# Second and third attention: value products in two column halves over two steps, maxima ahead of scores, outputs turned in the banks of the maxima

## The reference, cut to what matters

```python
# L1: EMBED 512, H = 32 heads, D = 16, 8 key/value heads, rope;  L2: 32 heads, D_K = 16, no rope, then a product with w_o
k = jnp.repeat(k, REP, axis=2)                                    # L1 only
scores = jnp.einsum('bqhd,bkhd->bhqk', q, k) / jnp.sqrt(jnp.float32(D))
probs = jax.nn.softmax(scores.astype(jnp.float32), axis=-1)
out = jnp.einsum('bhqk,bkhd->bqhd', probs, v).reshape(B, S, E)
```

## Time and profile before

| what | value |
|---|---|
| median of three executions | 2761.74 us |
| the profiled execution, its own time | 2762.35 us |
| its span, first to last instruction | 2760.6 us |
| TensorE busy / VectorE busy / ScalarE busy | 2230.8 / 1399.9 / 1264.6 us |
| mean granted clock of TensorE | 0.903 of full speed |
| L1 attention, its 256 steps | from 1194.87 us to 1593.45 us (last copy of O) |
| L2 attention, its 256 steps | from 1852.66 us to 2245.43 us |
| L2 attention, first and 13th copy of O | 1885.97 us, 2176.24 us |

### The profile page before, as it was taken

The page is one execution under the profiler, slowest core; times in us unless marked ns, Lnnn a source line. Parts: engine busy times, 40 slices in busy tenths (PEclk is TensorE's granted clock), DMA queues, the critical chain, the costliest instruction groups (busy, mean ns, idle before and its releaser), DMA issues. The chain is left out here.

```text
span 2760.6 us, 29801 instructions
## 1 busy us (share of the span) xinstructions
PE 2230.8 (81%) x10640; PEld 1250.1 (45%) x10640; DVE 1399.9 (51%) x1933; ACT 1264.6 (46%) x2097; POOL 630.0 (23%) x460
## 2 busy tenths in 40 slices
PE   4989999999997977478888757478888786998757
PEld 3657777777776733232222223222222233443434
DVE  3564545555552445577888163177888513103153
ACT  3545556556563222046777732017777742001321
POOL 1645655656552023200000022100000001001021
PEclk8989999999998988568999878789999988999878
DMA  4861111111112102302110002511121003000001
GB/s 106 245 206 39 46 57 54 42 57 54 43 42 89 61 22 90 77 1 36 18 26 10 1 16 91 129 17 24 30 41 24 1 16 123 0 0 0 18 12 47
DMA packets 78930, 138.70 MB, mean 50 GB/s; under 512 B 30808, under 2 KB 40792, under 8 KB 78832
## 3 DMA queue, kind: packets, MB, share of 16 engines
q1 hardware_dynamic: 78832, 137.40, 18.2%
HBM read 95.95 MB, written 41.03 MB: 50 GB/s over the span
## 5 line engine op out<-in xcount | busy, mean ns | idle before, releaser
L2139 POOL TENSOR_TENSOR l0a_p_low<-yT,l0a_p_high 128x1024 fp32r<-128x1024 f32 (+7 forms) x256 | 386.0, 1536 | 282.3 <-ACT l0a_p_high L2167 282.3
L173 POOL TENSOR_TENSOR applied<-prepared,neghalf 128x2 f32<-128x2 f32 x64 | 58.4, 913 | 1546.0 <-DVE prepared L154 1546.0
L1421 DVE TENSOR_REDUCE l2a_mx<-ps 128x2 f32<-128x1024 f32 x256 | 307.8, 1224 | 114.3 <-PE ps L1305 113.4
L1421 DVE TENSOR_REDUCE l1a_mx<-ps 128x2 f32<-128x1024 f32 x256 | 308.5, 1224 | 98.2 <-PE ps L1305 97.3
L1402 ACT ACTIVATE l1a_prob<-ps 128x512 f32<-128x512 f32 x512 | 278.0, 595 | 112.9 <-PE ps L1332 74.2
L1402 ACT ACTIVATE l2a_prob<-ps 128x512 f32<-128x512 f32 x512 | 278.0, 595 | 106.6 <-PE ps L1332 69.5
L2200 DVE TENSOR_REDUCE l0a_mx<-ps 128x1 f32<-128x512 f32 (+3 forms) x384 | 203.6, 553 | 236.2 <-PE ps L2046 145.3
L2156 ACT ACTIVATE yT<-ps 128x1024 f32<-128x1024 f32 (+7 forms) x256 | 166.3, 650 | 187.2 <-PE ps L2068 123.5
L1332 PE MATMUL ps<-l1a_q,l1a_k 49*128 49x512 f32 x512 | 135.0, 524 | 68.5 <-ACT l1a_prob L1402 64.4
L1332 PE MATMUL ps<-l2a_q,l2a_k 49*128 49x512 f32 x512 | 133.3, 518 | 69.1 <-ACT l2a_prob L1402 64.3
L2167 ACT CAST l0a_p_high<-yT 128x1024 fp32r<-128x1024 f32 (+7 forms) x256 | 172.6, 674 | 7.1
(11 more groups left out here) (297 smaller groups left out, 4233.4 us busy)
## 6 DMA issues: line engine op xcount, KB each, us to landing
l0a_q<-l0a_q SPq DMA_DIRECT2D x32, 512.0 KB, 3.3
l0q_woh<-in_l0a_wo SPq DMA_DIRECT2D x16, 512.0 KB, 5.2
l0a_q<-f SPq DMA_DIRECT2D x32, 256.0 KB, 4.6
l0a_q<-l0q_q_pe SPq DMA_DIRECT2D x32, 256.0 KB, 3.6
l0a_recip_rows<-l0a_recip_row SPq DMA_DIRECT2D x32, 256.0 KB, 3.4
l0a_o<-l0a_o_pair SPq DMA_DIRECT2D x16, 512.0 KB, 2.8
yT<-l0a_o SPq DMA_DIRECT2D x16, 512.0 KB, 3.3
l1a_q<-l1a_q_parts SPq DMA_DIRECT2D x16, 256.0 KB, 5.5
```

What stands on the lines that cost most here:

```text
L1421: nc.vector.tensor_reduce(mx[:, g % 2, :, p, qt, c], banks(("pair", m)), AX.X, ALU.max).then_inc(s_red, 1)
L2139: nc.gpsimd.tensor_tensor(p_low[:, j % 4, P * j:T], prob[:, j % 4, P * j:T], p_high[:, j % 4, P * j:T], ALU.subtract).then_inc(s_pl, 1)
```

## The change

Four things change in `attend`, for both attentions.

1. The four value products of a key tile are each cut into two of 256 columns. The first half stands in step 2j + 4 and the second in step 2j + 5, for j = 0 to 5; tile 6 has steps 16 and 17 and tile 7 has 17 and 18. So nearly each step has one half of a tile, where some had a whole one and others none.
2. In a step TensorE does the maxima first, then the turned maxima and the turned outputs where they are due, then it waits for the exponential and does the scores, then the value products.
3. The turned output goes into a pair of banks of the ring, and no more into `O`; it is a job of the ring, with its wait. It moves from step 20 to 21, and `finish` stays at 21. The next value products wait for the copy `osb` alone, no more for `finish`. The reciprocals get two buffers.
4. ScalarE copies `O` between the two exponentials of step 19, where it did so behind both.

```diff
--- before.py
+++ after.py
@@ -912,8 +912,8 @@
 EXT = MAX_ROW + 1
 AHEAD = 8
 TURN_STEP = STEPS - AHEAD + 2
-PV_STEP = (7, 8, 9, 10, 12, 14, 16, 18)
-OUT_STEP, TURN_OUT_STEP, FINISH_STEP = 19, 20, 21
+PV_STEP = [(2 * j + 4, 2 * j + 5) for j in range(6)] + [(16, 17), (17, 18)]
+OUT_STEP, TURN_OUT_STEP = 19, 21
 
 
 def rows_out(chip, name, W):
@@ -1164,7 +1164,7 @@
     mx = sb("mx", [P, 2, 2, 2, NT, 2])
     mcol = sb("mcol", [P, 4 * NT])
     mrow = sb("mrow", [4 * NT, P], F32R)
-    rden = sb("rden", [P, NT // 2, GROUP])
+    rden = sb("rden", [P, 2, NT // 2, GROUP])
     LOADS = 16 * 8
     loaded = [chip.shared(f"sa_heads_loaded{i}", LOADS * len(range(i, GROUPS, SLOTS))) for i in range(SLOTS)]
     placed = [chip.shared(f"sa_max_placed{i}", 32 * (GROUPS // 2)) for i in range(2)]
@@ -1206,6 +1206,9 @@
         if at >= 0 and at % STEPS == TURN_STEP and at // STEPS + 1 < GROUPS:
             turn_at[at // STEPS + 1] = at
             ring.append(("turn", at // STEPS + 1))
+        if at >= TURN_OUT_STEP and (at - TURN_OUT_STEP) % (2 * NT) == 0:
+            ring.append(("out", (at - TURN_OUT_STEP) // (2 * NT)))
+    ring.append(("out", GROUPS * HALVES - 1))
     ring_of = {job: r for r, job in enumerate(ring)}
 
     def banks(job):
@@ -1223,6 +1226,8 @@
         kind, n = ring[r]
         if kind == "pair":
             engine.wait_ge(s_red, b_red + n + 1)
+        elif kind == "out":
+            engine.wait_ge(s_out, b_out + n + 1)
         else:
             engine.wait_ge(s_mrow, b_mrow + n + 1)
 
@@ -1244,7 +1249,9 @@
     for g in range(GROUPS):
         for half in range(HALVES):
             for j in range(NT):
-                pv_at.setdefault(min((HALVES * g + half) * 2 * NT + PV_STEP[j], TOTAL - 1), []).append((g, half, j))
+                for c in range(2):
+                    at = (HALVES * g + half) * 2 * NT + PV_STEP[j][c]
+                    pv_at.setdefault(min(at, TOTAL - 1), []).append((g, half, j, c))
 
     def half_ended(at, lag):
 
@@ -1333,24 +1340,28 @@
                                           q[rows, slot, p, SPAN * half:SPAN * half + SPAN], start=True, stop=True)
                 mm.then_inc(s_st, 1)
 
-            def pv(g, half, j):
-                if j == 0 and (g or half):
-
-                    pe.wait_ge(s_out, b_out + HALVES * g + half)
-                if j == 0 and not (g or half):
+            def pv(g, half, j, c):
+                if j == 0 and c == 0 and (g or half):
+
+                    pe.wait_ge(s_oev, b_oev + HALVES * g + half)
+                if j == 0 and c == 0 and not (g or half):
                     pe.wait_ge(s_vout, b_vout + NT)
 
                 pe.wait_ge(s_exp, b_exp + 2 * ((HALVES * g + half) * 2 * NT + 2 * j + 2))
+                cut = slice(256 * c, 256 * c + 256)
                 for hh in range(GROUP):
-                    mm = nc.tensor.matmul(O[32 * hh:32 * hh + 32, :], vext[:, j, g * GROUP + hh if OWN_KEYS else g, :],
-                                          prob[:, j % 4, hh, :], start=j == 0, stop=j == NT - 1)
-                mm.then_inc(s_pv, 1)
+                    mm = nc.tensor.matmul(O[32 * hh:32 * hh + 32, cut], vext[:, j, g * GROUP + hh if OWN_KEYS else g, :],
+                                          prob[:, j % 4, hh, cut], start=j == 0 and c == 0,
+                                          stop=j == NT - 1 and c == 1)
+                if c == 1:
+                    mm.then_inc(s_pv, 1)
 
             def o_turn(n):
 
                 pe.wait_ge(s_oev, b_oev + n + 1)
+                wait_bank(pe, ("out", n))
                 for t in range(NT // 2):
-                    mm = nc.tensor.transpose(O[:, t * P:(t + 1) * P], osb[:, t * P:(t + 1) * P], chip.ident[:])
+                    mm = nc.tensor.transpose(banks(("out", n))[:, 0, t * P:(t + 1) * P], osb[:, t * P:(t + 1) * P], chip.ident[:])
                 mm.then_inc(s_ot, 1)
 
             for m in max_at[-1]:
@@ -1362,18 +1373,18 @@
             pe.wait_ge(s_vout, b_vout + NT)
             scores(0)
             for at in range(TOTAL):
+                for m in max_at.get(at, []):
+                    max_pair(m)
+                if turn_at.get(at // STEPS + 1) == at and at % STEPS == TURN_STEP:
+                    max_turn(at // STEPS + 1)
+                n = half_ended(at, TURN_OUT_STEP)
+                if n is not None:
+                    o_turn(n)
                 pe.wait_ge(s_exp, b_exp + 2 * at + 1)
                 if at + 1 < TOTAL:
                     scores(at + 1)
-                for m in max_at.get(at, []):
-                    max_pair(m)
-                n = half_ended(at, TURN_OUT_STEP)
-                if n is not None:
-                    o_turn(n)
                 for job in pv_at.get(at, []):
                     pv(*job)
-                if turn_at.get(at // STEPS + 1) == at and at % STEPS == TURN_STEP:
-                    max_turn(at // STEPS + 1)
             o_turn(GROUPS * HALVES - 1)
 
         @block.scalar
@@ -1401,9 +1412,9 @@
                 for hf in range(2):
                     nc.scalar.activation(prob[:, j % 4, 2 * p + hf, :], st(at, hf), ACT.Exp,
                                          scale=SCALE).then_inc(s_exp, 1)
-                n = half_ended(at, OUT_STEP)
-                if n is not None:
-                    o_out(n)
+                    n = half_ended(at, OUT_STEP)
+                    if hf == 0 and n is not None:
+                        o_out(n)
                 if at % STEPS == TURN_STEP + 1 and g + 1 < GROUPS:
                     max_out(g + 1)
             o_out(GROUPS * HALVES - 1)
@@ -1427,12 +1438,12 @@
             def finish(n):
                 g, half = divmod(n, HALVES)
                 dve.wait_ge(s_ot, b_ot + n + 1)
-                both = O.rearrange("p (t h e) -> p t h e", h=GROUP, e=2 * HD)
-                nc.vector.reciprocal(rden[:], both[:, :, :, HD]).then_inc(s_rd, 1)
+                both = banks(("out", n))[:, 0, :].rearrange("p (t h e) -> p t h e", h=GROUP, e=2 * HD)
+                nc.vector.reciprocal(rden[:, n % 2], both[:, :, :, HD]).then_inc(s_rd, 1)
                 dve.wait_ge(s_rd, b_rd + n + 1)
                 rows = f[:, half * (NT // 2):(half + 1) * (NT // 2), g * GROUP * HD:(g + 1) * GROUP * HD]
                 nc.vector.tensor_tensor(rows.rearrange("p t (h e) -> p t h e", e=HD), both[:, :, :, 0:HD],
-                                        rden[:].unsqueeze(3).broadcast_to([P, NT // 2, GROUP, HD]),
+                                        rden[:, n % 2].unsqueeze(3).broadcast_to([P, NT // 2, GROUP, HD]),
                                         ALU.mult).then_inc(s_out, 1)
 
             for m in max_at[-1]:
@@ -1442,7 +1453,7 @@
             for at in range(TOTAL):
                 for m in max_at.get(at, []):
                     reduce_pair(m)
-                n = half_ended(at, FINISH_STEP)
+                n = half_ended(at, TURN_OUT_STEP)
                 if n is not None:
                     finish(n)
             finish(GROUPS * HALVES - 1)
```

## The result

| | median us | runs | ratio to before, 95% interval |
|---|---|---|---|
| before, beside it | 2769.36 | 2758.88 to 2779.78, 4 | |
| changed | 2682.86 | 2682.05 to 2684.99, 4 | 0.9689 [0.9643, 0.9735] |

What follows compares the result with a forecast made beforehand. Bound: a latency ring of scores and exponential in one step, TensorE in the next. From 2762.35 us, 50.5 (L1) and 44.7 (L2) saved, 4 kept back for a clock fall, less 0.6: 2671; range 2650 to 2712.

Steps and rivals of the forecast that it cites:

- Part 1: Value products cut in halves: a half tile takes 0.56 us at full clock, where a whole tile took 0.99.
- The rival of issue-bound matmuls: Value products: four matmuls a pass keep 0.356 us, a half tile 0.28 dearer, 2816 us in all; chance 0.06.
- Part 2: Plain steps: TensorE sets 1.23 us with maxima, the ring of scores and exponential 1.19 without; before, 1.43 on average.
- The margin of 0.03 us: Plain step with maxima first: the exponential is ready at 1.42 us, the next scores' weights are wanted at 1.45.
- the second rival: Scores' weights behind maxima don't load ahead: plain steps take 1.42 us, 2733 in all, 2702 if in part; chance 0.10.
- Part 3: End of a half: copy step about 1.7 us, turned maxima 0.8 per group; a half with maxima takes 21.7.
- the 1.43: End of a half: ScalarE's stop of 1.43 us, as value products wait for `finish`, would go.
- Part 4: Starts and ends of an attention: 29.3 us to the first copy of O, 58.4 for the last three halves.
- At most one fall each: Both attentions: granted clock above 0.9, falling at most once in each.
- 4 us for the one that stays: Reserve in the sum for one remaining clock fall, sized by what one cost in L1 before, 7.7/2.
- The first rival: Both attentions: schedule gains as forecast but clock falls go on or move; 2691 us, up to 2705; chance 0.14.
- The fourth: Rival: evenly loaded steps keep the clock low, a half at 1.2 GHz taking 36 us against 21.7, slower; chance 0.04.

Runs made afterwards that it cites:

- the start prewarmed: Changed kernel with unread maxima pairs in the last 40 steps, turned maxima last, and unread matmuls ahead of step 0: 2679.13 us, ratio 0.9665.

## Why the prediction held, and where it was off

It said 2671.2 for the profiled execution, which took 2683.24: 12.0 more, inside the range. By its own steps:

- **Part 1, a half tile 0.56.** Right: 0.57. The split of the earlier trace rows into a part that scales with the clock and a fixed part held at half clock too (0.87 + 0.12 expected, 1.01 in the L2 rows above). The rival of issue-bound matmuls is out: it needed 0.28 us more a half, 0.84, and even with the fixed part counted in, a pass of four takes 0.57/2 = 0.29, under its 0.356. The second eight matmuls of step 17 cost 0.44 us, which is 0.22 a pass and 55 ns a matmul.
- **Part 2, the even step.** Right: 1.24 and 1.23 with maxima, 1.19 without. The margin of 0.03 us held, and the weights do load ahead, so the second rival is out. The rule of the Trainium skill that the prediction weighed ("TensorE: Matmul & The Clock Gate", Part 3), that a load overlaps running matmuls only when their row groups differ, does not hold here in that form: these loads begin 0.19 us after the maxima and are on the rows of the maxima. The prediction worked the margin out for maxima ahead of the wait. The step doesn't need that order: with scores first it is 1.24 as well.
- **Part 3, the end of a half.** A half of 21.7 came as 21.57: 21.2 without and 21.9 with turned maxima, so 0.72 per group for 0.8. The copy step was 1.57 for 1.7. The step ahead of it was 1.66 for 1.2, since its scores stand behind the two halves of step 17; the 16 x 1.23 of the sum has that work in it. The turned output's step was 2.02, for 1.23 + 0.59 + 0.1: each of maxima and scores takes 0.42 to 0.43 there instead of 0.33 or 0.34 (1317.75 to 1318.17, 1318.76 to 1319.19). Its new wait cost nothing, and the 1.43 is gone.
- **Part 4, starts and ends.** To the first copy 29.3 was too little: 34.5 and 30.8. Four steps of 2.16 were put at half clock; the traces had nine and five. The last three halves, 58.4, were 58.2 in L1 and 75.1 in L2.
- **The clock.** "At most one fall each" held, but 4 us for the one that stays did not. This is the term that was mis-sized: the length was taken from a fall of before (10.2 us), and the one that came lasted 51.2 and cost 16.7 (75.1 less 58.4). It came right behind steps 19 to 21 of a half without maxima. In the other three attentions profiled of the unedited kernel the same steps held the clock or lost it for 3.4 us only, so it is an event with a chance, not a property of the step. What starts it stays open. The first rival (the clock gives nothing back) is out for the twelve halves, which got back the 10.7 us that they had lost to it before, but it describes the end of L2. The fourth (evenness keeps the clock low) did not come for the kernel as a whole, but its mechanism showed, since evenly loaded steps, once at half clock, stayed there for 51.2 us here and for 30.7 with the start prewarmed.

In us: first copies +6.7, twelve halves twice -3.2, last three +16.5, the reserve of 4 not needed apart -4.0, the rest of the program -3.9: +12.1, the gap but for rounding. That the sum came so near is in part luck: its terms are 23.2 us too low and 11.1 too high, 3.9 of them in code that the change doesn't touch, and the same kernel profiled again took 2663.55, 8 under the forecast. The median of all ten executions of the changed kernel, 2682.3, is near the one profiled.

Which part gained, at full clock, for two halves: before 47.89, changed 43.14. Without the cut of the tiles 48.30, without the free bank 48.6, without the order 43.74. With the new order, neither the cut nor the bank gains without the other: the bank lets value products stand in nearly every step, and the cut makes a step of them fit.

## What to carry to other kernels

When one step of a pair is bound by a latency ring and the next by an engine, cut the engine's work so that each step has the same, and see first whether a buffer forces empty steps. Here the one without the other gave nothing. Price a clock fall not by the falls of the kernel before but by what every later step costs at the lower level, and keep it as a case with a chance: it took 16.7 us in one execution and 1.2 (59.5 less 58.3) in another. Read small edits by the distance of equal events in the trace at equal clock, over many of them (258.8, 258.2 and 257.6 us for twelve halves), since medians of four to six runs scatter by 10 us and untouched code alone moves by 19.
